# The last stage starts with a quarter of w1, each matmul waits for its own operand, and half of the inverse sums is made in attention's end

## The chip, the cores and the metric

One core of a Trainium2 chip runs the whole kernel. The metric is device microseconds from launch to end, as a median of runs.

## The reference, cut to what matters

```python
xn = layernorm(x)                                  # x: 4 x 2048 x 256
out = x + attention(xn) + moe(xn)
# attention: 16 heads of 16; out = softmax(q k) v; then @ Wo.T + bo
# moe(xn), 16 experts of 64 hidden units, top 2 of 16, then the 1024 best of 2048 tokens per expert and batch
h = gelu(xg @ w1 + b1)                             # xg: the tokens an expert keeps
outs = scatter_add(h @ w2 + b2)
z = xn + outs
moe = (z - mean(z)) / sqrt(var(z) + 1e-5) * gamma + beta
```

The kernel computes all experts on all tokens and multiplies by a mask, so gathering and scattering fall away.

## The kernel before, in words

Four stages, each a block of five instruction streams (PE, DVE, ACT, POOL, SP) that ends with a barrier: `norm` (line 155), `project` (346), `attend` (487) and `finish` (883).

`attend` goes through 64 heads (4 batches of 16). For a head it computes scores, their exponentials and the weighted values; row HD of each group of 32 rows is the softmax's sum. ACT copies the result to the tile `att`, and SP stores it to `att_dram` (`put_att`, line 655). DVE, after its last maxima, makes the 0/1 mask of tokens and experts in the unused part of `v_all` (lines 864 to 875); SP stores it to `mask_b` (707), issues the last head's store (709) and waits for it to land (710). That ends the block (its barrier is at line 563).

`finish` works in 16 blocks of 512 tokens. PE's order for a block, with expert pairs e = 0 to 7 (two experts fill 128 hidden units):
- `hide` (1045): six matmuls of 512 columns (two halves of the features, three products of rounded and remainder parts) into `h_ps`. It runs AHEAD = 2 pairs ahead of `unhide`.
- `unhide` (1059): twelve matmuls on w2 into `o_ps`.
- after pair 5 `hand_out` (1070) spreads the inverse sums over the head's features, and after pair 7 four matmuls add b2 (1103). `project` (1077) multiplies the previous block's attention by Wo.

Between hide and unhide a pair goes through ACT (Gelu, line 1131), DVE (`gate`, 1172, times the mask), ACT again (`g_hi`, 1134, rounded) and POOL (`g_lo`, 1297, the remainder). All buffers of this chain are double.

Ahead of block 0 the weights are prepared. SP loads w1 in four quarters of 256 KB (996), the first block's tokens as `xn_hi` and `xn_lo` (`halves`, 975; 512 KB each), w2 in two halves of 512 KB (999), masks, the sums of all heads (1002), the second block's halves, then waits for b2's split and loads the three parts of b2 (1008). ACT rounds each piece (1148), DVE takes the remainder (1245), POOL splits b2 and Wo (1286 to 1292). DVE then inverts all sums (1250) and splits the inverse into three bf16 parts, half by half, which SP stores to `inverse_dram` (1011). PE waits once, ahead of everything, for b2's rows, the spread matrix and Wo's parts (1106 to 1108).

SP's order for a block is `step` (1015): the halves of the next block, `quotients` (980, this block's attention numerators and inverses), then masks of this block and the next, with the tokens (968) between them. `masks(blk, q)` loads pairs 2q and 2q+1 in two DMAs into one of two buffers, each after the gates that last used it. SP issues in program order, so one wait holds all that stands behind it.

## Time and profile before

| | us |
|---|---|
| median of 3 runs | 3444.11 (3443.16 to 3446.69) |
| the profiled execution | 3444.21 |
| its span, first to last instruction | 3442.4 |
| busy: PE, DVE, ACT, POOL | 3296.2, 2894.2, 2526.4, 929.1 |
| mean granted clock of PE | 0.978 |

The span is what the profile shows of one execution. Of the timeline, stage `finish` runs from 2966.86 us to the end. Times of rows are from the span's start; "idle before <-" names what ended an engine's wait. A queue (SPq) row is the issue of a DMA, not its transfer.

### The profile page before, as it was taken

How to read it: one execution, taken by the hardware profiler on the slowest of the kernel's cores; microseconds unless marked ns; L12 is line 12 of the kernel's file. 1: busy time of each engine (PE TensorE's matmuls, PEld its weight loads, DVE VectorE, ACT ScalarE, POOL GpSimd, SP SyncE). 2: the span in 40 equal slices, each digit the busy share in tenths (PEclk: the TensorE clock that was granted, in tenths of full speed). 3: DMA queues.
4: the chain of work that ended last, by engine and by line, in shares of the span. 5: the costliest groups of instructions: out<-in, count | busy, mean ns of one | idle time of the engine just before them, and what ended most of it. 6: DMA issues, size and time to landing. Idle time of an engine off the chain costs nothing. (4 is left out here: it accounts for less than half of the span.)

```text
span 3442.4 us, 74610 instructions
## 1 busy us (share of the span) xinstructions
PE 3296.2 (96%) x20848; PEld 1706.4 (50%) x20848; DVE 2894.2 (84%) x2987; ACT 2526.4 (73%) x5726; POOL 929.1 (27%) x1339
## 2 busy tenths in 40 slices
PE   7868999999999999999999999999999999599998
PEld 6424444444444444444444444444444444288887
DVE  7508999999999999999999999999999998267777
ACT  3452888888888888888888888888888888443433
POOL 2550222222222222222222222222222222144443
PEclk9986999999999999999999999999999999799999
DMA  6581111122111211111121111211111121355553
GB/s 198 173 241 33 50 54 54 54 60 59 58 56 55 56 56 55 54 54 54 54 60 56 56 55 54 63 56 56 55 54 54 54 59 47 112 136 169 160 164 117
DMA packets 133063, 272.29 MB, mean 79 GB/s; under 512 B 22512, under 2 KB 68656, under 8 KB 120432
## 3 DMA queue, kind: packets, MB, share of 16 engines
q1 hardware_dynamic: 130464, 266.68, 26.7%
q8 instruction: 176, 2.88, 0.4%
q10 hardware_dynamic: 2256, 1.36, 0.2%
q14 instruction: 167, 1.37, 0.1%
HBM read 173.59 MB, written 84.93 MB: 75 GB/s over the span
## 5 line engine op out<-in xcount | busy, mean ns | idle before, releaser
L852 DVE TENSOR_REDUCE half_max<-m_ps 128x1 f32<-128x1024 f32 x2048 | 2413.4, 1220 | 324.5 <-PE m_ps L771 308.8
L724 ACT ACTIVATE prob<-s_ps 128x512 f32<-128x512 f32 (+1 forms) x5120 | 2188.3, 520 | 425.8 <-PE s_ps L781 423.2
L781 PE MATMUL s_ps<-q_feat,k_feat 50*128 50x512 f32 (+1 forms) x5120 | 1538.0, 396 | 7.5 <-issue 4.7
L771 PE MATMUL m_ps<-k_feat,q_feat 48*128 48x512 f32 x4096 | 1405.1, 448 | 55.9 <-DMA k_feat<-k_parts 28.4
L781 PEld LDWEIGHTS s_ps<-q_feat,k_feat 50*128 50x128 f32 x5120 | 796.2, 184 | 983.3 <-ACT prob L724 870.6
L790 PE MATMUL a_ps<-prob,v_head 128*32 128x512 f32 x8192 | 1091.6, 605 | 0.0
L771 PEld LDWEIGHTS m_ps<-k_feat,q_feat 48*128 48x128 f32 x4096 | 616.3, 187 | 287.5 <-DVE half_max L852 248.6
L579 POOL TENSOR_TENSOR shift<-row_max,shift 128x16 fp32r<-128x16 f32 x64 | 14.2, 222 | 1213.0 <-ACT shift L731 1213.0
L790 PEld LDWEIGHTS a_ps<-prob,v_head 128*32 128x32 f32 x8192 | 161.2, 108 | 253.7 <-issue 211.7
L1134 ACT ACTIVATE g_hi<-g 128x512 fp32r<-128x512 f32 x128 | 81.0, 632 | 243.8 <-DVE g L1172 199.8
L1297 POOL TENSOR_TENSOR g_lo<-g,g_hi 128x512 fp32r<-128x512 f32 x128 | 173.0, 1352 | 229.2 <-ACT g_hi L1134 229.2
L606 POOL TENSOR_SCALAR step_of<-route,cand 64x256 f32<-64x256 f32 x217 | 198.6, 915 | 44.5 <-POOL held L607 38.3
L573 POOL COPY v_head<-v_all 128x256 f32 (+1 forms) x64 | 25.3, 397 | 660.2 <-PE a_ps L790 660.1
L607 POOL TENSOR_TENSOR held<-held,step_of 64x256 f32<-64x256 f32 x217 | 157.6, 726 | 39.8 <-POOL step_of L606 39.8
L1172 DVE TENSOR_TENSOR g<-g,mask_bc 128x512 f32<-128x512 f32 x128 | 133.5, 1043 | 36.0 <-ACT g L1131 30.7
L1067 PE MATMUL o_ps<-w_hi,g_hi 128*128 128x256 f32 x512 | 144.6, 282 | 6.1 <-issue 3.7
L1067 PE MATMUL o_ps<-w_lo,g_hi 128*128 128x256 f32 x512 | 144.3, 282 | 0.0
L1067 PE MATMUL o_ps<-w_hi,g_lo 128*128 128x256 f32 x512 | 143.1, 280 | 0.0
L1056 PE MATMUL h_ps<-xn_hi,w_hi 128*128 128x512 f32 x256 | 105.7, 413 | 32.0 <-DMA b_rows<-b_parts 32.0
L1131 ACT ACTIVATE g<-h_ps,b_col 128x512 f32<-128x512 f32 x128 | 86.2, 674 | 25.7 <-PE h_ps L1056 25.7
L1067 PEld LDWEIGHTS o_ps<-w_hi,g_hi 128*128 128x128 f32 x512 | 96.5, 189 | 12.0 <-issue 7.1
L1056 PE MATMUL h_ps<-xn_lo,w_hi 128*128 128x512 f32 x256 | 102.1, 399 | 0.0
(132 smaller groups left out, 1904.1 us busy)
## 6 DMA issues: line engine op xcount, KB each, us to landing
q_feat<-q_parts SPq DMA_DIRECT2D x128, 256.0 KB
k_feat<-k_parts SPq DMA_DIRECT2D x128, 256.0 KB
q_parts<-parts SPq DMA_DIRECT2D x32, 512.0 KB, 4.8
k_parts<-parts SPq DMA_DIRECT2D x32, 512.0 KB, 4.8
q_feat<-q_parts SPq DMA_DIRECT2D x128, 128.0 KB
k_feat<-k_parts SPq DMA_DIRECT2D x128, 128.0 KB
att_dram<-att SPq DMA_DIRECT2D x64, 256.0 KB, 14.0
mask_bc<-mask_b SPq DMA_DIRECT2D x128, 128.0 KB, 4.4
```

The costliest lines, as they stand in the source:

```text
L606: do(pool.tensor_scalar(step_of[:, :], t["route"][:, c * PART:(c + 1) * PART], bound, None, ALU.is_ge))
L607: do(pool.tensor_tensor(held[:, :], held[:, :], step_of[:, :], ALU.add))
L724: act.activation(prob[tile(r, kt) % R][:, cols(j)], s_ps[slot(r, kt, j) % R][:, wide(j)], ACT.Exp).then_inc(exped, 1)
L771: ins = pe.matmul(m_ps[p % 2][:, k * BLK:(k + 1) * BLK], q_feat[r % 2][LOW, qt * P:(qt + 1) * P], k_feat[r % 2][LOW, key:key + BLK], start ...
L781: pe.matmul(s_ps[slot(r, kt, j) % R][:, wide(j)], k_feat[r % 2][UP, kt * P:(kt + 1) * P], q_feat[r % 2][UP, cols(j)], start=True, stop=Tru ...
L790: ins = pe.matmul(a_ps[qb * VW:(qb + 1) * VW, :], v_head[r % R][:, kt, :], prob[tile(r, kt) % R][:, qb * BLK:(qb + 1) * BLK], start=(kt == ...
L852: dve.tensor_reduce(half_max[r][:, p // 2, p % 2:p % 2 + 1], m_ps[p % 2][:, :], AX.X, ALU.max).then_inc(maxed, 1)
L1056: ins = pe.matmul(h_ps[e % 2][:, :], w, v, start=(c == 0 and k == 0), stop=(c == KC - 1 and k == 2))
L1067: ins = pe.matmul(o_ps[k], v, w[:, e, :], start=(e == 0 and m == 0), stop=False)
L1131: act.activation(g[e % 2][:, :], h_ps[e % 2][:, :], ACT.Gelu, bias=b1_col[:, e:e + 1]).then_inc(gelu, 1)
L1172: dve.tensor_tensor(g[e % 2][:, :], g[e % 2][:, :], mask_bc[q % 2][:, e % QTR, :], ALU.mult).then_inc(gated, 1)
L1297: pool.tensor_tensor(g_lo[e % 2][:, :], g[e % 2][:, :], g_hi[e % 2][:, :].bitcast(F32), ALU.subtract).then_inc(split, 1)
```

## The change

- `attend`: once 48 heads' values are copied and 32 heads are stored, SP loads the sums of the first 32 heads. DVE inverts and splits them after the mask, in `v_all` again, and SP stores the parts. The wait for the last head's store to land leaves `attend`; `att` and its semaphore are made outside the stage, and `finish` waits for it just before it loads the second half of the sums.
- `finish`: the pieces come in the order w1[0], w2[0], w1[1], w1[2], w2[1], w1[3]. SP loads w1[0], the first halves, w2[0], masks(0, 0), the other pieces, masks(0, 1), quotients(0), tokens(0); then it waits for b2's split and loads b2, the sums' second half and halves(1, 1).
- ACT and DVE take three pieces ahead of block 0 and one more after each of its pairs 0 to 2. ACT's warming Gelu stands after the three; it rounds Wo after pair 4. DVE inverts the second half after pair 4 and splits it after pair 5; SP stores it after block 0's step and waits for the store.
- POOL splits b2 after pair 1 and Wo after pair 5 of block 0.
- PE waits for the spread matrix in `hand_out`, for Wo in `project`, for b2 ahead of the b2 matmuls, and in hide and unhide for the pieces by their new places.

```diff
@@ -122,6 +122,8 @@
         minus_half = sb("minus_half", [P, TPB])
+        att = sb("att", [P, BLK])
+        att_out = sem("a_att_out")
@@ -530,7 +532,8 @@
     att_read = sem("a_att_read")
-    att_out = sem("a_att_out")
+    att_out = t["att_out"]
+    sums_in, inv_chain, inverted, inverse_stored = sem("a_sums_in"), sem("a_inv_chain"), sem("a_inverted"), sem("a_inverse_stored")
     staged = sb("staged", [P, BLK], F32R)
@@ -544,6 +547,8 @@
     mask16 = spare[0:B * E, 3 * S:3 * S + S // 2].bitcast(BF16)
+    sums = spare[:, 4 * S:4 * S + BLK]
+    inv_parts = spare[:, 4 * S + BLK:4 * S + BLK + PARTS * BLK // 2].bitcast(BF16).rearrange("p (k s) -> p k s", k=PARTS)
     TREE = 8
@@ -698,6 +703,9 @@
                     step(i * U + r, r, half=i * (U // 2) + (r - 1) // 2)
+            sp.wait_ge(v_ready, (B - 1) * H)
+            sp.wait_ge(att_out, 16 * (P // BPS + 1))
+            sp.dma_start(sums, sum_rows(t, 0)).then_inc(sums_in, 16)
             for g in range(1 + ROUNDS * U, HEADS):
@@ -705,9 +713,12 @@
             sp.dma_start(t["mask_b"], mask16).then_inc(mask_stored, 16)
+            sp.wait_ge(inverted, 1)
+            sp.dma_start(t["inverse_dram"][0:P], inv_parts).then_inc(inverse_stored, 16)
             sp.wait_ge(mask_stored, 16)
+            sp.wait_ge(inverse_stored, 16)
+            sp.wait_ge(att_out, 16 * HEADS)
             put_att(HEADS - 1)
-            sp.wait_ge(att_out, 16 * (HEADS + 1))
@@ -873,6 +884,14 @@
             dve.tensor_copy(mask16, gt).then_inc(masked, 1)
+
+            dve.wait_ge(sums_in, 16)
+            do = Chain(dve, inv_chain)
+            do(dve.reciprocal(sums, sums))
+            for k in range(PARTS - 1):
+                do(dve.tensor_copy(inv_parts[:, k, :], sums))
+                do(dve.tensor_tensor(sums, sums, inv_parts[:, k, :], ALU.subtract))
+            dve.tensor_copy(inv_parts[:, PARTS - 1, :], sums).then_inc(inverted, 1)
@@ -925,8 +944,11 @@
     w2_raw = [sb(f"w2_raw{k}", [P, EP // 2, D]) for k in range(2)]
-    pieces = [*([(w1_raw[q], w1_hi[:, :, w1_cols[q]], w1_lo[:, :, w1_cols[q]])] for q in range(4)),
-              *([(flat(w2_raw[k]), *(flat(w)[:, k * 2 * BLK:(k + 1) * 2 * BLK] for w in (w2_hi, w2_lo)))] for k in range(2))]
+    w1_pieces = [(w1_raw[q], w1_hi[:, :, w1_cols[q]], w1_lo[:, :, w1_cols[q]]) for q in range(4)]
+    w2_pieces = [(flat(w2_raw[k]), *(flat(w)[:, k * 2 * BLK:(k + 1) * 2 * BLK] for w in (w2_hi, w2_lo))) for k in range(2)]
+    pieces = [w1_pieces[0], w2_pieces[0], w1_pieces[1], w1_pieces[2], w2_pieces[1], w1_pieces[3]]
+    W1_AT, W2_AT = (0, 2, 3, 5), (1, 4)
+    AHEAD_PIECES = 3
     piece_in = [sem(f"e_piece_in{k}") for k in range(len(pieces))]
@@ -992,25 +1014,30 @@
             w2_rows = t["w2"].rearrange("(c p) n -> p c n", p=P)
-            for q in range(4):
-                sp.dma_start(w1_raw[q], w1_rows[:, :, w1_cols[q]]).then_inc(piece_in[q], 16)
+
+            def load_w1(q):
+                sp.dma_start(w1_raw[q], w1_rows[:, :, w1_cols[q]]).then_inc(piece_in[W1_AT[q]], 16)
+
+            def load_w2(k):
+                sp.dma_start(w2_raw[k][:, :, :], w2_rows[:, 4 * k:4 * k + 4, :]).then_inc(piece_in[W2_AT[k]], 16)
+
+            load_w1(0)
             halves(0, 0)
-            for k in range(2):
-                sp.dma_start(w2_raw[k][:, :, :], w2_rows[:, 4 * k:4 * k + 4, :]).then_inc(piece_in[4 + k], 16)
+            load_w2(0)
             masks(0, 0)
-            for half in range(2):
-                sp.dma_start(sums[:, half, :], sum_rows(t, half)).then_inc(sums_in, 16)
+            load_w1(1)
+            load_w1(2)
+            load_w2(1)
+            load_w1(3)
             masks(0, 1)
+            quotients(0)
             tokens(0)
-            halves(1, 1)
             sp.wait_ge(b2_split, 1)
...
                 sp.dma_start(b2_rows[k * E:(k + 1) * E, :], b2_parts[:, k, :]).then_inc(b2_placed, 16)
-            for half in range(2):
-                sp.wait_ge(sums_inverted, half + 1)
-                sp.dma_start(t["inverse_dram"][half * P:(half + 1) * P], inv_parts[:, :, :]).then_inc(inverses_stored, 16)
-                sp.wait_ge(inverses_stored, 16 * (half + 1))
-            quotients(0)
+            sp.wait_ge(t["att_out"], 16 * (HEADS + 1))
+            sp.dma_start(sums[:, :], sum_rows(t, 1)).then_inc(sums_in, 16)
+            halves(1, 1)
@@ -1030,6 +1057,9 @@
             step(0, 0, first=True)
+            sp.wait_ge(sums_inverted, 1)
+            sp.dma_start(t["inverse_dram"][P:2 * P], inv_parts[:, :, :]).then_inc(inverses_stored, 16)
+            sp.wait_ge(inverses_stored, 16)
             with sp.Fori(0, NBLK // 2 - 1) as i:
@@ -1046,7 +1076,7 @@
                     pe.wait_ge(xn_in[u], (blk // 2 + 1) * 32)
-                pe.wait_ge(piece_split, 1 + e // 2)
+                pe.wait_ge(piece_split, 1 + W1_AT[e // 2])
                 pe.wait_ge(gelu, n + 1)
@@ -1057,7 +1087,7 @@
             def unhide(blk, u, e):
-                pe.wait_ge(piece_split, 5 + e // 4)
+                pe.wait_ge(piece_split, 1 + W2_AT[e // 4])
                 pe.wait_ge(split, blk * EP + e + 3)
@@ -1068,6 +1098,7 @@
             def hand_out(blk):
+                pe.wait_ge(spread_chain, 4)
                 pe.wait_ge(num_in, (blk + 1) * 16 * NUM_LOADS)
@@ -1075,6 +1106,7 @@
             def project(blk):
+                pe.wait_ge(wo_split, 1)
                 pe.wait_ge(num_split, blk + 1)
@@ -1098,14 +1130,12 @@
                         hand_out(blk)
+                pe.wait_ge(b2_placed, 16 * PARTS)
                 pe.wait_ge(loaded, (blk + 1) * 48)
...
-            pe.wait_ge(b2_placed, 16 * PARTS)
-            pe.wait_ge(spread_chain, 4)
-            pe.wait_ge(wo_split, 1)
             for e in range(AHEAD):
@@ -1120,7 +1150,6 @@
             act.dma_start(woT_sb[:, :, :], t["woT"].rearrange("(c p) n -> p c n", p=P)).then_inc(wo_in, 16)
-            act.activation(t["warm"][:, :], t["ident"][:, 0:1], ACT.Gelu)
             act.sem_inc(gelu, 2)
@@ -1133,30 +1162,34 @@
-            def block_step(blk, u, following=True):
+            def round_piece(k):
+                src, hi, lo = pieces[k]
+                act.wait_ge(piece_in[k], 16)
+                act.activation(hi, src, ACT.Copy).then_inc(piece_rounded, 1)
+
+            def block_step(blk, u, first=False):
                 for e in range(EP):
                     hidden_units(blk, e)
+                    if first and AHEAD_PIECES + e < len(pieces):
+                        round_piece(AHEAD_PIECES + e)
+                    if first and e == 4:
+                        act.wait_ge(wo_in, 16)
+                        act.activation(wo_hi[:, :, :], woT_sb[:, :, :], ACT.Copy).then_inc(wo_rounded, 1)
                     if e == EP - 1:
...
             act.sem_inc(projected, 2)
-            for k, piece in enumerate(pieces):
-                act.wait_ge(piece_in[k], 16 * len(piece))
-                for src, hi, lo in piece:
-                    ins = act.activation(hi, src, ACT.Copy)
-                ins.then_inc(piece_rounded, 1)
-                if k == 1:
-                    act.wait_ge(wo_in, 16)
-                    act.activation(wo_hi[:, :, :], woT_sb[:, :, :], ACT.Copy).then_inc(wo_rounded, 1)
+            for k in range(AHEAD_PIECES):
+                round_piece(k)
+            act.activation(t["warm"][:, :], t["ident"][:, 0:1], ACT.Gelu)
             act.wait_ge(small_in, 16 * 3)
-            act.wait_ge(piece_split, 5)
-            block_step(0, 0)
+            block_step(0, 0, first=True)
             with act.Fori(0, NBLK // 2 - 1) as i:
...
                     block_step(i * 2 + 1 + u, 1 - u)
-            block_step(NBLK - 1, 1, following=False)
+            block_step(NBLK - 1, 1)
@@ -1220,9 +1253,32 @@
+            def split_piece(k):
+                src, hi, lo = pieces[k]
+                dve.wait_ge(piece_rounded, k + 1)
+                dve.tensor_tensor(lo, src, hi.bitcast(F32), ALU.subtract).then_inc(piece_split, 1)
+
+            do = Chain(dve, inv_chain)
+
+            def invert_sums():
+                dve.wait_ge(sums_in, 16)
+                do(dve.reciprocal(sums[:, :], sums[:, :]))
+
+            def split_inverses():
+                for k in range(PARTS - 1):
+                    do(dve.tensor_copy(inv_parts[:, k, :], sums[:, :]))
+                    do(dve.tensor_tensor(sums[:, :], sums[:, :], inv_parts[:, k, :], ALU.subtract))
+                dve.tensor_copy(inv_parts[:, PARTS - 1, :], sums[:, :]).then_inc(sums_inverted, 1)
+
             def gates(blk, u, last=True, following=True):
...
                     gate(blk, e)
+                    if not last and AHEAD_PIECES + e < len(pieces):
+                        split_piece(AHEAD_PIECES + e)
+                    if not last and e == 4:
+                        invert_sums()
+                    if not last and e == 5:
+                        split_inverses()
                     if last and e == AHEAD - 1:
@@ -1239,24 +1295,8 @@
-            for k, piece in enumerate(pieces):
-                dve.wait_ge(piece_rounded, k + 1)
-                for src, hi, lo in piece:
-                    ins = dve.tensor_tensor(lo, src, hi.bitcast(F32), ALU.subtract)
-                ins.then_inc(piece_split, 1)
-            dve.wait_ge(small_in, 16 * 3)
-            dve.wait_ge(sums_in, 32)
-            do = Chain(dve, inv_chain)
-            do(dve.reciprocal(sums[:, :, :], sums[:, :, :]))
-            for half in range(2):
-                if half:
-                    dve.wait_ge(inverses_stored, 16)
-                left = sums[:, half, :]
-                for k in range(PARTS - 1):
-                    do(dve.tensor_copy(inv_parts[:, k, :], left))
-                    do(dve.tensor_tensor(left, left, inv_parts[:, k, :], ALU.subtract))
-                dve.tensor_copy(inv_parts[:, PARTS - 1, :], left).then_inc(sums_inverted, 1)
-            dve.wait_ge(piece_split, 6)
+            for k in range(AHEAD_PIECES):
+                split_piece(k)
             gates(0, 0, last=False)
@@ -1281,16 +1321,6 @@
             pool.wait_ge(spread_chain, 4)
-            pool.wait_ge(small_in, 16 * 3)
-            chain = Chain(pool, b2_chain)
-            chain(pool.tensor_copy(b2_parts[:, 0, :], b2_sb[:, :]))
-            chain(pool.tensor_tensor(b2_left[:, :], b2_sb[:, :], b2_parts[:, 0, :], ALU.subtract))
-            chain(pool.tensor_copy(b2_parts[:, 1, :], b2_left[:, :]))
-            pool.tensor_tensor(b2_parts[:, 2, :], b2_left[:, :], b2_parts[:, 1, :], ALU.subtract).then_inc(b2_split, 1)
-            pool.wait_ge(b2_split, 1)
-            pool.wait_ge(wo_rounded, 1)
-            pool.tensor_tensor(wo_lo[:, :, :], woT_sb[:, :, :], wo_hi[:, :, :].bitcast(F32), ALU.subtract).then_inc(wo_split, 1)
-
             def split_units(blk, e):
@@ -1302,11 +1332,29 @@
+            def split_b2():
+                pool.wait_ge(small_in, 16 * 3)
+                chain = Chain(pool, b2_chain)
+                chain(pool.tensor_copy(b2_parts[:, 0, :], b2_sb[:, :]))
+                chain(pool.tensor_tensor(b2_left[:, :], b2_sb[:, :], b2_parts[:, 0, :], ALU.subtract))
+                chain(pool.tensor_copy(b2_parts[:, 1, :], b2_left[:, :]))
+                pool.tensor_tensor(b2_parts[:, 2, :], b2_left[:, :], b2_parts[:, 1, :], ALU.subtract).then_inc(b2_split, 1)
+                pool.wait_ge(b2_split, 1)
+
+            def split_wo():
+                pool.wait_ge(wo_rounded, 1)
+                pool.tensor_tensor(wo_lo[:, :, :], woT_sb[:, :, :], wo_hi[:, :, :].bitcast(F32), ALU.subtract).then_inc(wo_split, 1)
+                pool.wait_ge(wo_split, 1)
+
             def block_step(blk, last=True):
...
                         invert(blk - 1)
+                    if not last and e == 1:
+                        split_b2()
+                    if not last and e == 5:
+                        split_wo()
```

## Rows read from the trace of the kernel before

**Rows 1.** The page's first part: engine, busy time, share of the span, instructions.

```profile
PE 3296.2 (96%) x20848; PEld 1706.4 (50%) x20848; DVE 2894.2 (84%) x2987; ACT 2526.4 (73%) x5726; POOL 929.1 (27%) x1339
```

**Rows 2.** Timeline of PE: its first matmuls of the last stage, and the second block's start.

```profile
2993.30 0.80 PE L1056 MATMUL h_ps<-xn_hi,w_hi 128*128 128x512 f32 x1 [32.03 <-DMA b_rows<-b_parts]
...
3003.72 0.36 PE L1067 MATMUL o_ps<-w_hi,g_hi 128*128 128x256 f32 x1 [3.66 <-issue]
...
3027.24 0.61 PE L1103 MATMUL o_ps<-b_rows,mask_rows 48*128 48x256 bf16 x4
```

**Rows 3.** Windows: us, busy PE, PEld, DVE, ACT, POOL, granted clock, DMA share, GB/s.

```profile
2966.80:2973.30 6.50, 0.00 (x0) 0.00 (x0) 1.01 (x2) 2.74 (x4) 1.70 (x4) 0.50 0.56 161
2973.30:2983.20 9.90, 0.00 (x0) 0.00 (x0) 2.95 (x4) 2.72 (x4) 3.35 (x5) 0.50 1.05 328
2993.30:2996.50 3.20, 3.20 (x8) 2.52 (x9) 2.38 (x5) 0.10 (x1) 0.00 (x0) 0.50 0.00 0
3054.60:3081.35 26.75, 26.75 (x176) 23.71 (x175) 19.77 (x30) 10.73 (x18) 12.35 (x11) 1.00 0.61 163
```

**Rows 4.** Instructions of line 563 (attention's end) and line 193 (first stage's end).

```profile
L563 SPq COMPARE_BRANCH  x1: 49/49/49, 2964.0 to 2964.0; - x1
L563 SPq DRAIN  x1: 68/68/68, 2966.6 to 2966.6; - x1
...
L193 ACTq DRAIN  x1: 1496/1496/1496, 92.8 to 92.8; - x1
```

**Rows 5.** Timeline of SP's queue: attention's last store, then the last stage.

```profile
2962.02 0.34 SPq L657 DMA_DIRECT2D att_dram<-att  x1
2966.86 1.95 SPq L996 DMA_DIRECT2D w_raw<-in_w  x4
...
2969.36 1.94 SPq L978 DMA_DIRECT2D xn_lo<-tok_all  x1
...
2981.65 1.86 SPq L1008 DMA_DIRECT2D b_rows<-b_parts  x3
...
3005.58 19.06 SPq L965 DMA_DIRECT2D mask_bc<-mask_b  x8
```

**Rows 6.** DMA issues of three narrow windows: KB each, us from issue to landing.

```profile
xn_lo<-tok_all SPq DMA_DIRECT2D x1, 512.0 KB, 10.1
...
xn_lo<-tok_all SPq DMA_DIRECT2D x1, 512.0 KB, 6.7
...
mask_bc<-mask_b SPq DMA_DIRECT2D x1, 128.0 KB, 5.3
```

**Rows 7.** Timeline of ACT in the last stage's beginning.

```profile
2968.87 1.28 ACT L1123 ACT_TABLE_LOAD   x1 [6.94 <-issue]
2970.16 0.20 ACT L1123 ACTIVATE warm<-ident 128x1 f32<-128x1 f32 x1
2970.89 0.63 ACT L1148 ACTIVATE w_hi<-w_raw 128x512 fp32r<-128x512 f32 x1 [0.53 <-DMA w_raw<-in_w]
```

**Rows 8.** Timeline of DVE: mask chain's end, first split, the inverses, first gate.

```profile
2925.06 1.22 DVE L875 CAST v_all<-v_all 64x2048 bf16<-64x2048 f32 x1
2971.55 0.69 DVE L1245 TENSOR_TENSOR w_lo<-w_raw,w_hi 128x512 fp32r<-128x512 f32 x1 [45.27 <-ACT w_hi L1148]
...
2986.43 6.55 DVE L1250 RECIPROCAL sums<-sums 128x1024 f32<-128x1024 f32 x1 [0.65 <-DMA sums<-att_dram]
...
2995.39 0.43 DVE L1258 CAST inv_parts<-sums 128x512 bf16<-128x512 f32 x1
...
3000.94 0.68 DVE L1172 TENSOR_TENSOR g<-g,mask_bc 128x512 f32<-128x512 f32 x1
```

**Rows 9.** Timeline of POOL: the first and the fourth instruction that split b2.

```profile
2975.57 0.39 POOL L1286 CAST b_parts<-b_sb 16x256 bf16<-16x256 f32 x1 [6.79 <-DMA gamma_bc<-in_gamma]
...
2977.23 0.66 POOL L1289 TENSOR_TENSOR b_parts<-b_left,b_parts 16x256 bf16<-16x256 f32 x1
```

**Rows 10.** Waits of SP's queue, 2955 to 3030 us: total, times, longest.

```profile
SPq L656 <- ACT att L736: 28.0, 1, 28.0
```

4 lines of the change are left out of this document (2 added, 2 removed).

## The prediction

> **What bounds the kernel now.** I read the page's first part first: PE is busy 96% of the span, all other engines less [rows 1]. So time comes off only where PE stands still, or where it waits in the chain. PE's own timeline shows one large hole: its first matmul of the last stage starts at 2993.30 after 32.03 us of idleness [rows 2]. Behind it the last stage is a stream: between 3054.60 and 3081.35 PE is busy 26.75 of 26.75 us, and that is one block [rows 3]. All of the change lies in the hole and in the first block behind it; the other 15 blocks end as much earlier as the first one does.
>
> What ends the hole: PE waits for all three b2 rows. Their DMAs are issued from 2981.65 [rows 5] and stand behind everything issued before. What would end it next, if each matmul waited only for its own operand, is the question. Two marks serve for the sum: PE's first matmul on w2 at 3003.72, and the b2 matmul that ends block 0's sums at 3027.24 [rows 2]. Between them lie 23.5 us. The last stage starts at 2966.86 with SP's first load [rows 5]. I call the new start T and count from there.
>
> **The barrier.** SP issues attention's last store at 2962.02 for 0.34 us, waits for its landing, branches at 2964.0 and only reaches its drain at 2966.6 [rows 4, 5]. The change drops the wait for the landing. The 2.8 us from the branch to the first load stay. T = 2962.36 + 2.8 = 2965.2, a gain of 1.7. Bounds: 0 (something else holds the barrier) and 4.3 (the 2.6 us before the drain go too). I take 1.7, since the landing is what the trace has in front of the branch.
>
> **First operands.** Before, xn_lo was issued sixth, behind 1.05 MB of w1 and the 0.5 MB of xn_hi, and landed 10.1 us after its issue, 12.6 after the start [rows 5, 6]. Now it is third, issued near T+1. Lower bound: in the running stage the same load lands after 6.7 us [rows 6], so T+7.7. Upper: T+12.6. I take T+9.2: 1.7 MB (first w1 quarter, both halves of xn, ACT's 0.4 MB) at a rate between the 161 and 328 GB/s of the two windows [rows 3], and the 2 us that attention's last store needed to land. The first w1 quarter was rounded at 2970.89, T+4.0, and split by T+5.4 [rows 7, 8], earlier. PE's clock is granted at 0.50 there, 1.2 GHz, with 8 matmuls in 3.2 us [rows 3]; it will be after 13 us of idleness as well. Two hides of six matmuls take 2.6 us each: the first ends at T+11.8.
>
> **ACT's order is the next bound.** ACT now rounds three pieces (w1's first quarter, w2's first half, w1's second) before the Gelu table is loaded. Behind xn_lo come w2's half, two masks and that quarter, 1.05 MB: at 328 GB/s [rows 3] 3.2 us, so T+12.4. Rounding takes 0.63; the table load and the warming instruction span 2968.87 to 2970.36, 1.5 us [rows 7]. Before, these hid behind the first landing; now they lie on the path. First Gelu at T+14.5, its end and the first gate at T+15.2. From the first gate to the first w2 matmul took 3000.94 to 3003.72, 2.8 us [rows 2, 8]. So the first w2 matmul comes at T+18.0 = 2983.2, which is 20.5 us earlier than before.
>
> The load's row shows 1.28 us and the next instruction 0.01 us behind it [rows 7], but it came after ACT had issued DMAs, not behind running work. The Trainium skill (ScalarE: Activation LUTs, What ACT_TABLE_LOAD costs) counts a drain of some 1.4 us beside it, 2.66 us for each switch of set. By it, this load behind three roundings would cost that much more than the row, and the whole time would be 1.4 us longer. No row here has a drain beside a load, so the sum goes by the row.
>
> **Block 0, new waits.** ACT and DVE each take one more piece after the first three experts. A step is gate 0.7, g_hi 0.63, rounding 0.63, Gelu 0.7 and some 0.3 of hand-overs: 3.0 us. The w2 half is twice as wide, rounding and split some 1.1 and 1.2 (doubled from 0.63 and 0.69 less a fixed part [rows 7, 8]): 3.9. Gates stand at T+15.2, 18.2, 22.1, 25.1; the fifth would follow at T+27.5.
>
> It won't, because SP is held. SP waits for b2's split before it loads b2's rows, the sums, the second block's halves and then the masks of experts 4 and 5. POOL splits b2 only after its second g_lo, which ends near T+21.1. The four instructions take 2975.57 to 2977.89, 2.3 us [rows 9]: T+23.4. SP then needs 1.9 for b2 [rows 5], 0.5 for the sums, 1.1 for the halves: the two masks are issued from T+27.0. With 1 MB just ahead of them they land late: the row for a mask behind halves says 5.3 us after issue [rows 6], xn_lo's 10.1 behind a full backlog is the other end. I take 6.0 after the second issue: T+33.6. Everything SP issued before (some 5.3 MB) needs about 20 us at these rates and is through by then. So **the fifth gate waits some 6 us for its masks**, a wait that kernel before does not have (its SP was free at 3005.58 [rows 5]).
>
> After it, DVE inverts the second half of the sums: half of 6.55, 3.3 us, then, after the next gate, the split of 2992.98 to 2995.82, 2.8 us [rows 8]. Gates: T+33.7, 38.0, 41.8, and 44.6 behind the division. The eighth w2 group starts at T+47.4, takes 1.4 and the b2 matmul comes at T+48.9 = 3014.1 (before: 3027.24). The gain is **13.1 us**; of the 20.5, 7.4 are given back in block 0 (6 by the masks, the rest by the inversion and the pieces). POOL's split of wo (1.3 us, after the sixth g_lo) fits into the slack of a 2.8 us step.
>
> **At nothing.** In attention's end one DMA more reads the sums and one stores the inverses; SP waits 28.0 us there for ACT's last copy [rows 10], and DVE is idle 45.27 us behind its mask chain [rows 8] for 3.3 + 2.8 of new work. Were that cover gone, 6 us would be due. PE's three waits per block that stood once ahead of the blocks: its sequencer runs ahead of matmuls in a stream that is busy 26.75 of 26.75 us with waits in every group [rows 3], so 0. If they cost, 48 waits at 0.05 us are 2.4. The start-up issues (18 against 19 ahead of the b2 wait) end by T+14 and hide before T+23.4. Behind block 0 SP stores the inverses and waits some 3 us: last masks out at T+46, landed inverses T+49, halves and quotients T+52.6, the next masks issued by T+53.9 and landed 5.3 later at T+59.2. They are wanted 4/8 of 26.75 = 13.4 us after the block's start, T+62.3. Hidden, by 3 us; if that fails it is a rival below.
>
> **Sum.** The profiled execution took 3444.21 us, span 3442.4 and 1.8 around it, 0.1 above the median 3444.11. 3444.2 less 13.1 is 3431.1; I forecast 3431.
>
> **Rivals.**
> (a) No mask wait: the masks land before T+28, as POOL comes to b2 sooner or the queues are empty. For it: 5.3 us is a loaded landing. Against: SP's own issues put them at T+27 already. The inversion of the sums stays. Gain 5 more: 3426.
> (b) ACT drains before it switches tables. Where ACT ended a stage behind running work, its drain took 1.50 us [rows 4]; one of these on the path gives 3432.6. For it stands that the load now follows ACTIVATEs; against, that the load's row shows nothing around it. The Trainium skill's rule above is this rival, at nearly the same price.
> (c) Late operands: xn_lo at its upper bound T+12.6 and all behind it 3.4 later; or PE, busy in short bursts, stays at 1.2 GHz [rows 3] through block 0. Gain 8 to 10: 3435.
> (d) Both (c) and a mask landing like the 10.1 of a full backlog: 3444.2 - 13.1 + 3.4 + 4.1 = 3438.6, no change.
> (e) Slower: SP stays late. It runs through one fixed order per block, masks behind halves and quotients; if its 3 us of lateness isn't caught up, the fifth gate of every block waits. Break-even is 13.1 / 15 = 0.9 us per block; at 1.5 it gives 3453.6. Against it: the eight mask loads of block 0 span 19.06 us of SP's time [rows 5], of which issuing is 8 x 0.6; the rest is waiting for gates and absorbs 3 us.
> That the change doesn't do what it says would be PE's first matmul still waiting for b2; the moved waits exclude it.
>
> **How the numbers follow.** Forecast 0.50, (a) 0.15, (b) 0.10, (c) 0.12, (d) 0.08, (e) 0.05. A measurement can tell 0.2%, 6.9 us. (a), (b), (c) and the forecast are faster by more: 0.87. Same 0.08, slower 0.05. The range goes from 3424 (a, with the earlier barrier) to 3437 (c at its worst), leaving out (d), (e) and the tails.
>
> **What would show it.** Right: the last stage starts near 2965.2; PE's first matmul there 9 us later, no longer released by the b2 rows; first w2 matmul near 2983; a table load between third rounding and first Gelu; the fifth gate of block 0 idle some 6 us, ended by a mask DMA; a reciprocal of 128x512 with 3.3 us behind it; the b2 matmul near 3014; then 26.75 us per block. Wrong: no idle time before the fifth gate (a); blocks above 26.75 us (e); PE still at 0.50 after T+20 (c).

## The result, and the profile after

| | before | after |
|---|---|---|
| median, one comparison | 3445.11 (3443.16 to 3447.10, 12 runs) | 3437.53 (3433.69 to 3440.66, 12 runs) |
| profiled execution | 3444.21 | 3436.23 |
| its span | 3442.4 | 3434.5 |

The ratio is 0.9977, interval 0.9969 to 0.9986: 7.6 us faster (interval 4.8 to 10.7), by more than the 0.2% that can be told, where I had 13.1. The time lies 0.5 us above the end of my range.

The same marks as in the prediction: T is SP's first load of the last stage, gates and the b2 matmul of block 0 are counted from T, "stage" is the span less T, and "block 1" goes from block 0's b2 matmul to the next one.

| | forecast | after | before |
|---|---|---|---|
| T | 2965.2 | 2963.72 | 2966.86 |
| PE's first matmul | +9.2 | +8.4 | +26.4 |
| first gate | +15.2 | +15.6 | +34.1 |
| first w2 matmul | +18.0 | +18.5 | +36.9 |
| fifth gate | +33.7 | +35.6 | +45.1 |
| b2 matmul of block 0 | +48.9 | +52.2 | +60.4 |
| block 1 | 26.75 | 29.81 | 26.75 |
| stage | 464.1 | 470.8 | 475.5 |

The start went as forecast. The stage is 6.7 us longer than forecast: 3.3 us of it arose in block 0, behind the fourth gate, 3.1 in block 1, where I had put nothing, and the rest behind it.

**The start.** PE's timeline, changed kernel; to be held against [rows 2]:

```profile
2972.08 0.79 PE L1086 MATMUL h_ps<-xn_hi,w_hi 128*128 128x512 f32 x1 [12.79 <-DMA xn_lo<-tok_all]
...
2982.21 0.55 PE L1097 MATMUL o_ps<-w_hi,g_hi 128*128 128x256 f32 x1
...
3015.87 0.61 PE L1136 MATMUL o_ps<-b_rows,mask_rows 48*128 48x256 bf16 x4
```

xn_lo now ends the hole, and the hole is 12.79 instead of 32.03 us. ACT's timeline there, against [rows 7]:

```profile
2976.49 0.63 ACT L1168 ACTIVATE w_hi<-w_raw 128x512 fp32r<-128x512 f32 x1 [0.68 <-DMA w_raw<-in_w]
2977.14 1.28 ACT L1186 ACT_TABLE_LOAD   x1
2978.44 0.20 ACT L1186 ACTIVATE warm<-ident 128x1 f32<-128x1 f32 x1
2978.55 0.67 ACT L1160 ACTIVATE g<-h_ps,b_col 128x512 f32<-128x512 f32 x1
```

The rounding ends at 2977.12 and the table load starts at 2977.14; nothing stands between them. The Trainium skill (ScalarE: Activation LUTs, What ACT_TABLE_LOAD costs) counts a drain of some 1.4 us beside a load of 1.28; the trace agrees on the load and shows no drain.

**The fifth gate.** SP's queue, against [rows 5]:

```profile
2960.05 0.33 SPq L662 DMA_DIRECT2D att_dram<-att  x1
2963.72 0.40 SPq L1019 DMA_DIRECT2D w_raw<-in_w  x1
...
2988.93 1.86 SPq L1037 DMA_DIRECT2D b_rows<-b_parts  x3
...
2992.55 20.59 SPq L987 DMA_DIRECT2D mask_bc<-mask_b  x8
3013.18 0.59 SPq L1061 DMA_DIRECT2D inverse_dram<-inv_parts  x1
3017.44 0.41 SPq L998 DMA_DIRECT2D xn_hi<-tok_hi_dram  x1
```

POOL's timeline of the same moments, against [rows 9]:

```profile
2985.25 1.38 POOL L1338 CAST b_parts<-b_sb 16x256 bf16<-16x256 f32 x1
2986.71 1.00 POOL L1339 TENSOR_TENSOR b_left<-b_sb,b_parts 16x256 f32<-16x256 f32 x1
```

And DVE's, against [rows 8]:

```profile
2979.32 0.69 DVE L1205 TENSOR_TENSOR g<-g,mask_bc 128x512 f32<-128x512 f32 x1 [1.48 <-ACT g L1160]
...
2984.91 1.47 DVE L1259 TENSOR_TENSOR w_lo<-w_raw,w_hi 128x1024 fp32r<-128x1024 f32 x1 [1.65 <-ACT w_hi L1168]
...
2999.32 0.69 DVE L1205 TENSOR_TENSOR g<-g,mask_bc 128x512 f32<-128x512 f32 x1 [8.19 <-DMA mask_bc<-mask_b]
2999.93 3.34 DVE L1265 RECIPROCAL sums<-sums 128x512 f32<-128x512 f32 x1
...
3005.09 1.38 DVE L1269 CAST inv_parts<-sums 128x512 bf16<-128x512 f32 x1
3006.51 1.66 DVE L1270 TENSOR_TENSOR sums<-sums,inv_parts 128x512 f32<-128x512 f32 x1
...
3028.99 0.69 DVE L1205 TENSOR_TENSOR g<-g,mask_bc 128x512 f32<-128x512 f32 x1 [3.33 <-issue]
```

The predicted wait for masks is there, 8.2 us. SP asks for the fifth gate's masks at T+28.8 (forecast T+27.0), since POOL's split of b2 took 3.65 us, from 2985.25 to 2988.90, instead of 2.3: its first cast took 1.38 instead of 0.39 and ended within 0.3 us of DVE's w_lo subtraction. The landings are right to a tenth: 5.3 and 6.0 us after their issues from 2992.55 on (the DMA view of that moment gives the median of the two), and the gate runs as the second lands:

```profile
mask_bc<-mask_b SPq DMA_DIRECT2D x2, 128.0 KB, 5.7
```

**Block 1.** The last DVE row is the one that I had not foreseen. It is block 1's fourth gate. It waits 3.33 us for nothing that a semaphore shows, and PE runs dry behind it. Windows of block 1 and block 2 of the changed kernel (us, busy PE, PEld, DVE, ACT, POOL, clock, DMA share, GB/s):

```profile
3015.90:3045.70 29.80, 27.02 (x176) 23.55 (x176) 19.81 (x30) 10.60 (x18) 12.30 (x10) 1.00 0.54 149
3045.70:3072.40 26.70, 26.70 (x175) 23.69 (x174) 19.77 (x30) 10.68 (x18) 12.36 (x10) 1.00 0.57 163
```

It happens once: in block 2 PE is busy throughout again. Block 1 is the first block that the engines run from their loops (`Fori`); block 0's code stands ahead of them. The DMA view lists a queue "q14 instruction" that carries code. Its first packet of block 1, in the kernel before (3035.7 to 3036.0, 8.6 us behind the b2 matmul):

```profile
DMA packets 1, 0.01 MB, mean 27 GB/s; under 512 B 0, under 2 KB 0, under 8 KB 0
q14 instruction: 1, 0.01, 7.5%
```

and in the changed kernel (3026.8 to 3027.1, 11.1 us behind it):

```profile
DMA packets 36, 0.04 MB, mean 137 GB/s; under 512 B 3, under 2 KB 35, under 8 KB 35
q1 hardware_dynamic: 35, 0.03, 50.8%
q14 instruction: 1, 0.01, 9.8%
```

Before, it moves alone, over queues already empty. After, it comes 2.5 us later and among 35 data packets: those of block 2's halves and block 1's quotients and masks, which SP issues from 3017.44 on, 1.6 us behind the b2 matmul, where it was 2.2 us ahead of it before. From the b2 matmul to the stall, DVE's own instructions stand at the same distance from that matmul in both kernels, within 0.2 us. SP is that late because it stores the inverses at 3013.18 and waits for the landing. The gate starts 2.0 us after the packet. That the gate waits for this packet is read from their times; no row names it as the releaser. The Trainium skill (Runtime: NRT & Kernel Launch, Instruction fetch mechanics) says that each engine fetches its code in blocks of 16 KiB over a DMA queue of its own, and that crossing from one block to the next is mostly hidden. Block 1 has two packets of 0.01 MB on that queue, in line with the size; hidden it was in the kernel before, and not here, where DVE stood still for 3.33 us.

### The profile page after: what moved, and what is told of

It is laid out like the page before. It is cut to its first block and busy times, and to the rows that moved or that the text cites. A ratio compares the mean times of both kernels' runs of the same rounds, so it can differ in the third digit from the quotient of the medians.

```text
span 3434.5 us, 74611 instructions
## 1 busy us (share of the span) xinstructions
PE 3299.8 (96%) x20848; PEld 1708.6 (50%) x20848; DVE 2898.2 (84%) x2988; ACT 2525.7 (74%) x5726; POOL 932.6 (27%) x1339
## 5 line engine op out<-in xcount | busy, mean ns | idle before, releaser
L584 POOL TENSOR_TENSOR shift<-row_max,shift 128x16 fp32r<-128x16 f32 x64 | 14.3, 223 | 1211.2 <-ACT shift L742 1211.2
L1097 PE MATMUL o_ps<-w_hi,g_hi 128*128 128x256 f32 x512 | 145.6, 284 | 13.7 <-POOL g_lo L1327 13.7
L1086 PE MATMUL h_ps<-xn_hi,w_hi 128*128 128x512 f32 x256 | 106.1, 414 | 15.3 <-DMA xn_lo<-tok_all 12.8
L1086 PE MATMUL h_ps<-xn_hi,w_lo 128*128 128x512 f32 x256 | 102.0, 398 | 0.0
```

What stands on the lines that cost most here:

```text
L1086: ins = pe.matmul(h_ps[e % 2][:, :], w, v, start=(c == 0 and k == 0), stop=(c == KC - 1 and k == 2))
L1097: ins = pe.matmul(o_ps[k], v, w[:, e, :], start=(e == 0 and m == 0), stop=False)
```

## The experiments

Theory A: the forecast's mechanism holds; 2 to 3 us were lost in block 0 to POOL's late b2 split and DVE's slowed inversion split, and 3 in block 1 to late code behind late data. Rival B: block 1's hole is a fixed cost of the new code's length or place. Rival C: the barrier or PE's added waits cost what is missing.

All results; rows in one group ran beside the same runs of the kernel before. The stage is that of each profiled execution.

| run | median | ratio (interval) | first gate | fifth gate | b2 matmul | block 1 | stage |
|---|---|---|---|---|---|---|---|
| before: 3446.47 | | | | | | | |
| changed, again | 3440.02 | 0.9979 (0.9970, 0.9988) | 15.7 | 34.9 | 51.4 | 30.46 | 470.3 |
| store early | 3437.10 | 0.9971 (0.9960, 0.9982) | 15.3 | 35.8 | 52.4 | 27.14 | 469.3 |
| b2 early | 3433.26 | 0.9963 (0.9949, 0.9976) | 15.4 | 30.7 | 47.3 | 29.04 | 464.9 |
| warm first | 3437.81 | 0.9972 (0.9961, 0.9982) | 14.0 | 33.1 | 49.6 | 31.33 | 469.4 |
| before: 3446.76 | | | | | | | |
| before, again | 3446.33 | 0.9999 (0.9989, 1.0009) | 34.1 | 44.0 | 58.9 | 26.75 | 474.9 |
| waits only | 3446.47 | 1.0001 (0.9992, 1.0011) | 34.5 | 46.5 | 61.8 | 26.75 | 477.2 |
| masks first | 3432.49 | 0.9955 (0.9941, 0.9969) | 16.3 | 28.4 | 45.5 | 31.06 | 465.5 |
| landing kept | 3440.62 | 0.9979 (0.9970, 0.9988) | 17.0 | 37.3 | 53.8 | 28.79 | 471.1 |
| before: 3446.64 | | | | | | | |
| reordered | 3427.89 | 0.9946 (0.9933, 0.9960) | 14.4 | 26.6 | 43.7 | 26.93 | 459.0 |
| sums inverted first | 3429.48 | 0.9950 (0.9937, 0.9964) | 17.1 | 29.3 | 43.7 | 26.79 | 460.2 |
| stored twice | 3442.07 | 0.9984 (0.9975, 0.9993) | 15.9 | 35.7 | 52.3 | 30.44 | 471.7 |
| before: 3445.70 | | | | | | | |
| sums second | 3426.18 | 0.9942 (0.9929, 0.9956) | 16.4 | 28.5 | 42.9 | 26.76 | 458.7 |

Attention's end moves by up to 5.5 us from one execution to the next (PE's last matmul there ends between 2959.29 and 2964.78), whatever the kernel. So a theory is judged by the stage, and by medians only with their intervals.

The stage moves too, by PE's granted clock. In the last block PE stands still for 2.40 us in all fourteen profiles. Behind that hole it is granted 2.4 GHz throughout in some and 1.2 for a while in others, and the same block takes 26.61 or up to 27.85 us. Windows of the last block of the version with all reorderings and of the one with the store early, and of block 1 of the changed kernel's repeat:

```profile
3385.38:3411.99 26.61, 24.21 (x163) 21.52 (x162) 18.99 (x29) 10.05 (x16) 12.31 (x10) 1.00 0.33 104
```

```profile
3391.74:3419.59 27.85, 25.45 (x164) 22.67 (x163) 18.99 (x29) 10.03 (x16) 12.30 (x10) 0.95 0.30 99
```

```profile
3019.21:3049.67 30.46, 28.54 (x175) 24.99 (x175) 19.19 (x30) 10.82 (x18) 12.29 (x10) 0.94 0.52 145
```

Block 1 was granted 0.94 or 0.95 in three profiles (changed again, warm first, masks first), behind PE holes of 1.9 to 2.8 us, and 1.00 in all others, one with a hole of 3.4 us among them. In the repeat's block 1 PE was busy for 28.54 us, in the first profile's for 27.02, with as many matmuls within one. So 1.2 to 1.5 us of a block in a single profile can be the clock and not the edit.

**Both kernels again.** No edit.

> The changed kernel once more, for a second profile. Theory A (code of DVE comes late because the data transfers of block 1 come late, a thing of the program's order): the idle 3.3 us with no releaser ahead of DVE's gate of pair 3 in block 1 is there again, within 1 us, and PE loses some 2.8 us to it. Theory B (chance of one execution): it is not there, or at another place. Both expect the fifth gate of block 0 to wait 8 us for its masks, and a time near 3437.5.

> The kernel before once more, for a second profile. If attention itself varies from one execution to the next, its last matmul ends up to 2 us away from 2961.3, as it did in the five profiles of the changed kernels (2959.3 to 2963.8), while the stage behind it takes 475.5 within 0.5. If the kernel before has DVE's idle time without a releaser in block 1 too, it shows here; I expect none, and blocks of 26.75 from the second on.

Stages repeat: 470.8 and 470.3, 475.5 and 474.9, in part by luck: in the kernel before, block 0 took 1.5 us less the second time and the last block 0.9 more. Block 1 is longer both times in the changed kernel, by 3.06 and 3.71 us. DVE's stall was 3.33 us and then 2.48; the second time 1.5 us of the 3.71 are the clock's. The stage gives 4.8 us of the gain; the barrier gives 1.2. In the changed kernel's first profile PE left attention 2.0 us earlier than in the first of before, which no edit explains; the two repeats are 0.3 us apart.

**PE's waits alone.** On the kernel before:

```diff
             def hand_out(blk):
+                pe.wait_ge(spread_chain, 4)
...
             def project(blk):
+                pe.wait_ge(wo_split, 1)
...
                         hand_out(blk)
+                pe.wait_ge(b2_placed, 16 * PARTS)
...
-            pe.wait_ge(b2_placed, 16 * PARTS)
-            pe.wait_ge(spread_chain, 4)
-            pe.wait_ge(wo_split, 1)
```

> The kernel before with one part of the change alone: PE waits for b2, the spread matrix and Wo where it uses them, and no longer ahead of everything. Theory 1 (the three waits are what holds PE 32 us): PE's first matmul comes with xn_lo, near T+12.7 instead of T+26.4, and the stage is up to 13 us shorter. Theory 2 (DVE holds the first gate: it ran at 3000.94, right behind the last cast of the inverses at 2995.82 and 3001.0, and no PE wait changes that): the first matmul is as early as in theory 1, but the first gate stays at T+34.1, the first w2 matmul at T+36.9, and the whole time within 1 us of before (3446).

Nothing is gained: 1.0001. PE's and DVE's timelines of that kernel:

```profile
2981.51 0.80 PE L1056 MATMUL h_ps<-xn_hi,w_hi 128*128 128x512 f32 x1 [18.38 <-DMA xn_lo<-tok_all]
...
3006.05 0.55 PE L1067 MATMUL o_ps<-w_hi,g_hi 128*128 128x256 f32 x1 [16.87 <-issue]
```

```profile
3002.91 0.43 DVE L1258 CAST inv_parts<-sums 128x512 bf16<-128x512 f32 x1
3003.26 0.68 DVE L1172 TENSOR_TENSOR g<-g,mask_bc 128x512 f32<-128x512 f32 x1
```

PE's first matmul comes 13.7 us earlier, and the first gate at T+34.5 as ever, directly behind the last cast of the inverses. So "PE waits for all three b2 rows" names what ended PE's hole and not what bounded the stage: that was DVE's program order, inverses ahead of gates. The change gains by moving the inversion; that the waits had to move with it is argued, since no run moves the inversion alone. The 48 added waits leave the blocks from block 1 on at 26.75 (the last at 26.71).

The stage is even 1.7 to 2.2 us longer. PE starts early, then stands still for 16.87 us, and is granted 1.2 GHz behind it, where the kernel before had 0.80 and 1.00 in the same stretch of its two profiles:

```profile
3003.30:3011.70 8.40, 5.65 (x20) 5.10 (x21) 3.14 (x4) 3.20 (x6) 3.81 (x3) 0.50 0.44 141
```

**The landing kept.** On the changed kernel, at attention's end:

```diff
             put_att(HEADS - 1)
+            sp.wait_ge(att_out, 16 * (HEADS + 1))
```

> The changed kernel, with the wait for the last store's landing back in attention's end. From that store's issue to the last stage's first load it was 4.84 us before and 3.67 and 3.69 in the two profiles after. If the removed wait is what made the difference, it is 4.8 again and the time is 1.2 us longer than the changed kernel (3441); if the 2.5 us of SP ahead of its drain overlap with the landing in another way, it stays at 3.7.

SP's queue, with the wait:

```profile
2964.52 0.33 SPq L662 DMA_DIRECT2D att_dram<-att  x1
2969.33 0.40 SPq L1020 DMA_DIRECT2D w_raw<-in_w  x1
```

From the last store to the first load: 4.81 us with the wait (4.84, 4.90 and 4.92 in the three profiles of before and of the waits alone), 3.67 and 3.69 in the changed kernel. The barrier's part is 1.2 us. In the medians it does not stand out (ratios 0.9979 and 0.9979).

**The store of the inverses ahead of the last masks:**

```diff
                 for q in range(4):
+                    if q == 3 and first:
+                        sp.wait_ge(sums_inverted, 1)
+                        sp.dma_start(t["inverse_dram"][P:2 * P], inv_parts[:, :, :]).then_inc(inverses_stored, 16)
...
-            sp.wait_ge(sums_inverted, 1)
-            sp.dma_start(t["inverse_dram"][P:2 * P], inv_parts[:, :, :]).then_inc(inverses_stored, 16)
             sp.wait_ge(inverses_stored, 16)
```

> SP stores the second half's inverses ahead of the last two mask loads of block 0, so that the landing is over when they are issued, and block 1's halves, quotients and masks go out some 3 us earlier. Theory A: DVE's idle time of 3.3 us with no releaser in block 1 goes, PE streams through block 1 without its 2.8 us hole, and the time falls by 2.8 us (3434.7). Theory B (the hole does not depend on SP's order): hole and time stay within 1 us (3437.5). A third: the last masks of block 0 are now late, block 1 waits for them, and the time rises.

Its gate in block 1, and the code packet (3025.2 to 3025.5, 8.7 us behind the b2 matmul, near the 8.6 of the kernel before):

```profile
3027.22 0.70 DVE L1206 TENSOR_TENSOR g<-g,mask_bc 128x512 f32<-128x512 f32 x1 [0.63 <-issue]
```

```profile
q14 instruction: 1, 0.01, 6.4%
```

SP is 2.3 us ahead of the b2 matmul again, the packet moves alone, the stall falls from 3.33 to 0.63, block 1 from 29.81 and 30.46 to 27.14. Rival B falls: the code is as long and, but for these lines, in the same place. Of these 3 us the stage of this profile keeps 1.3, as its last block took 27.85 us at a granted clock of 0.95; the median lies 2.9 us below the changed kernel's beside it.

The fourteen profiles fall into two groups. In seven (the kernel before twice, waits only, store early, reordered, and both with the sums inverted ahead) SP issues block 2's halves 2.2 to 2.3 us ahead of the b2 matmul, the packet comes 8.5 to 8.7 us behind it, and block 1 takes 26.75 to 27.14. In the other seven SP issues them 1.4 to 4.3 us behind it, the packet comes 10.1 to 11.7 us behind it, DVE stalls for 2.3 to 4.0 us, and block 1 takes 28.79 to 31.33.

**The inverses stored twice** (SP made later on purpose):

```diff
             sp.wait_ge(inverses_stored, 16)
+            sp.dma_start(t["inverse_dram"][P:2 * P], inv_parts[:, :, :]).then_inc(inverses_stored, 16)
+            sp.wait_ge(inverses_stored, 32)
```

> The changed kernel, with the store of the inverses and the wait for its landing done twice behind block 0: 3 us more of lateness of SP. Theory A: block 1's halves, quotients and masks go out 3 us later, DVE's idle time without a releaser grows from 2.5 to 3.3 us to some 6, block 1 from 29.8 to 30.5 to some 33, and the time by 2 to 3 us (3441). Theory B (not SP's order): block 1 as in the changed kernel, time the same. If instead the gates of block 1 wait for a mask DMA by name, the lateness acts through the masks and not through code.

Waits of DVE in block 1 (total, times, longest):

```profile
DVE g L1207 <- issue: 4.0, 1, 4.0
```

SP's loads come 4.3 us behind the b2 matmul instead of 1.6, the packet 11.7 us behind it instead of 11.1, the stall is 4.0, the longest of all, and block 1 takes 30.44. That is no longer than in the changed kernel's repeat, but there 1.5 us were the clock's; of the late profiles with a granted clock of 1.00 (28.79, 29.04, 29.81) it is longer by 0.6 us or more. The gate again starts 2.1 us after the packet. Direction right, size well short: the packet is not held until SP's data are through, since those now end 1 to 2 us after it. In all nine profiles with a stall the gate starts 1.7 to 2.1 us after the packet. That SP's order makes the stall is shown by the edits; that it does so through the code is inferred from these times, and by what rule data delay the packet stays open.

**b2 split ahead of POOL's first g_lo:**

```diff
-                    if not last and e == 1:
-                        split_b2()
...
+            split_b2()
             block_step(0, last=False)
```

> POOL splits b2 ahead of block 0, as before the change; all else is the changed kernel. Theory of the prediction (SP is held by the wait for b2's split, and the masks of pairs 4 and 5 go out late): SP passes the wait by T+14, those masks are issued right after the second gate, near T+20, the fifth gate's wait of 8.2 us falls under 1 us, and the whole time by 5 to 7 us (3431). Rival (the transfers themselves are the bound, SP's wait only hides it): the masks land no earlier than T+32, the wait moves by 2 us at most, the time by under 2 us.

```profile
2997.32 0.69 DVE L1205 TENSOR_TENSOR g<-g,mask_bc 128x512 f32<-128x512 f32 x1 [4.49 <-DMA mask_bc<-mask_b]
```

The fifth gate and the b2 matmul come 4.1 to 4.9 us earlier, and the stage is 5.6 us shorter. The rest of the wait, 4.5 us, is not POOL's: the masks are asked for from 19.3 us after T on, and land 7.5 and 10.6 us after their issues, behind 1 MB of the second block's halves and what was queued before it. (The 9.1 that the next expectation names is the median of the two.)

**b2 early, and those halves and tokens behind the fifth gate's masks:**

```diff
             quotients(0)
-            tokens(0)
...
-            halves(1, 1)
...
                         masks(blk + q // 2, (q + 2) % 4)
+                    if q == 0 and first:
+                        halves(1, 1)
+                        tokens(0)
```

> The kernel with b2 split early, and beside it SP loads the masks of pairs 4 and 5 ahead of the first block's tokens and the second block's halves (2.1 MB). With b2 alone split early these masks went out 9.5 us sooner, yet their landing took 7.5 to 9.1 us and the fifth gate still waited 4.5 us, at T+30.7. Theory (queue: what SP issued ahead of them holds them): they land some 4 us after issue, near T+24, the fifth gate is at T+28 without a wait, and the stage is 2.7 us shorter than with b2 alone (462.2 against 464.9 from T to the end); the whole time near 3431. Rival (DVE is late in any case): the fifth gate stays within 0.5 us of T+30.7, and nothing is gained.

No wait for masks is left; the fifth gate follows the fourth after 2.0 us. The b2 matmul comes at T+45.5, 1.7 us earlier than with b2 alone, yet the stage is no shorter: block 1 took 31.06 instead of 29.04. The stall accounts for 0.6 of these 2.0 us (3.17 after 2.57); PE's clock, granted at 0.95 in this block and at 1.00 in the other, for 1.5. The expected 2.7 us are neither shown nor excluded: against their own runs of before the medians gained 14.3 and 13.2.

**The warming Gelu ahead of the pieces:**

```diff
             act.sem_inc(projected, 2)
+            act.activation(t["warm"][:, :], t["ident"][:, 0:1], ACT.Gelu)
             for k in range(AHEAD_PIECES):
                 round_piece(k)
-            act.activation(t["warm"][:, :], t["ident"][:, 0:1], ACT.Gelu)
```

> The warming Gelu stands ahead of the three pieces, as before the change. If ACT's order was the bound of the first gate, as predicted, table load and warming (1.5 us) hide behind the first landing, the first gate comes at T+14.1 instead of T+15.6, and by the forecast the whole time falls by up to 1.5 us. Rival: the fifth gate waits for its masks in any case, SP's issue of them hangs on POOL's second g_lo and moves with it by 1.5, so block 0 ends 1.5 earlier; if instead the masks' landing is bound by transfers, block 0 ends where it did and the time stays within 0.5 us.

```profile
2970.20 1.28 ACT L1184 ACT_TABLE_LOAD   x1 [5.76 <-issue]
2971.50 0.20 ACT L1184 ACTIVATE warm<-ident 128x1 f32<-128x1 f32 x1
...
2980.69 0.64 ACT L1168 ACTIVATE w_hi<-w_raw 128x512 fp32r<-128x512 f32 x1 [0.78 <-DMA w_raw<-in_w]
2981.24 0.66 ACT L1160 ACTIVATE g<-h_ps,b_col 128x512 f32<-128x512 f32 x1
```

The first Gelu stands directly behind the third rounding and the first gate at T+14.0, 1.6 us earlier: the 1.5 us that the prediction put on the path. With a drain it would have been 3. Block 1 is the longest seen, at 31.33, with the same stall of 3.33 us as in the changed kernel's first profile and a granted clock of 0.95.

**All four reorderings together** (store, b2, masks and Gelu as above, without the doubled store).

> Four reorderings of the changed kernel together, each tried alone or in a pair before: b2 split ahead of block 0, masks of pairs 4 and 5 ahead of tokens and second halves, inverses stored ahead of the last masks, warming Gelu first. Theory A (DVE's code comes late because block 1's data go out late): the idle time without a releaser in block 1 falls under 1 us, block 1 takes under 27.5 us (31.1 with the first two alone), and with the first gate 1.6 us earlier the stage from T to the end is near 461 (465.5 with the first two alone); the time near 3428. Theory B (the hole comes from DVE's place in its code, however early data go): block 1 stays at 29 to 31 us, the stage near 464, the time near 3431.

The two windows are its block 1 and block 2:

```profile
3010.66:3037.60 26.94, 26.94 (x176) 23.57 (x175) 19.84 (x30) 10.64 (x18) 12.32 (x10) 1.00 0.58 158
3037.60:3064.35 26.75, 26.75 (x176) 23.71 (x175) 19.76 (x30) 10.74 (x18) 12.36 (x10) 1.00 0.56 162
```

3427.9 is 18.8 us below the kernel before. The stage is 11.5 us shorter than the changed kernel's (470.5, the mean of two), and the parts one by one gave only 7.5: 1.3 the store, 5.6 b2, 1.2 the Gelu, and the masks on top of b2 a loss of 0.6. That looks as if they helped one another, but a good part is the clock: 1.2 us of the store's last block, and 1.5 of block 1 in the Gelu's and the masks' profiles. By medians the parts add up. Beside the changed kernel's 3440.02 the store gave 2.9, b2 6.8 and the Gelu 2.2, and the masks 1.1 on top of b2, 13.0 in all; together they gave 12.3 beyond the repeat's 6.5. No run shows more than a sum.

**The sums inverted before the first gate.** As all four, but SP loads the sums behind xn and stores their inverses behind b2, and DVE inverts them after its first piece:

```diff
             halves(0, 0)
+            sp.wait_ge(t["att_out"], 16 * (HEADS + 1))
+            sp.dma_start(sums[:, :], sum_rows(t, 1)).then_inc(sums_in, 16)
...
-            for k in range(AHEAD_PIECES):
+            split_piece(0)
+            invert_sums()
+            split_inverses()
+            for k in range(1, AHEAD_PIECES):
                 split_piece(k)
```

> As the four reorderings, but the second half of the sums is loaded behind xn and inverted by DVE ahead of block 0, between its first and second piece, where DVE waits for data. Then the gates of pairs 5 and 6 lose the 1.2 and 2.4 us by which they exceed 2.8, block 0 is 3 us shorter behind its first gate; the 256 KB ahead of w2 and the second w1 quarter make the first gate up to 1.5 later. Net 1 to 3 us faster than the reordered kernel (3425 to 3427). Rival: the split of the inverses ends later than the second piece is rounded, so the first gate is 3 us later and nothing is gained.

A miss. The sums were in DVE's hands only at T+9.2, the inverses done at T+15.4, and the first gate came at T+17.1. From first gate to b2 matmul it is 26.6 us instead of 29.3, as the inversion is out of the stream; the two cancel, and the b2 matmul comes at T+43.7 in both. The stage's other 1.2 us are its last block, 27.85 at a granted clock of 0.94.

**The same, the sums loaded ahead of xn** (the two added lines stand above `halves(0, 0)`).

> T is the issue of SP's first load of the last stage. As the version with the sums inverted first, but the sums (256 KB) go out ahead of xn instead of behind its first two pieces. If what cost that version 2.6 us at the first gate was the late landing of the sums (T+9.2), they now land near T+5.5 and are inverted by about T+12, beside the wait for the second piece: first gate near T+15.4, block 0 behind it 26.6 us as there, its b2 matmul near T+42, the stage 457 to 458 us, the time near 3426. Rival: the sums ahead delay xn, w2 and the second quarter by 1 us or more, or the inversion still ends behind the second piece: first gate at T+16.5 or later, the stage 459 to 460 us, the time 3428 to 3429.5, no better than the four reorderings together.

PE's first matmul, and DVE's last cast of the inverses:

```profile
2977.22 0.80 PE L1087 MATMUL h_ps<-xn_hi,w_hi 128*128 128x512 f32 x1 [15.81 <-DMA xn_lo<-tok_all]
```

```profile
2976.72 0.77 DVE L1272 CAST inv_parts<-sums 128x512 bf16<-128x512 f32 x1
```

The inverses are ready at T+11.8, as expected, but 256 KB ahead of xn cost PE's first matmul 3.3 us (T+11.5) and the first gate 2.0. The rival was right on the delay, the expectation on block 0 (26.6 behind the gate), and the stage of 458.7 lies between the two. The time of 3426.2 came out as expected, but in the profiled execution 1.2 us of it is attention's earlier end; the stage is 0.3 us shorter than with the four reorderings, and the ratios 0.9942 and 0.9946 can't be told apart. Either is the best version.

## Why the prediction was off, step by step

- **What bounds the kernel**: half right. PE's hole was where the time lay, but removing its wait alone gains nothing; DVE's inversions ahead of the gates held the stage at T+34.
- **The barrier**: 1.2 us instead of 1.7; inside its bounds.
- **First operands, ACT's order**: right. T+8.4 for 9.2, first gate T+15.6 for 15.2, w2 T+18.5 for 18.0. The table load cost its 1.3 us with no drain, so rival (b) falls, and with it, for this load, the figure of the Trainium skill. Windows of PE's clock, in the changed kernel:

```profile
2984.00:2999.30 15.30, 10.36 (x62) 8.38 (x60) 4.99 (x4) 4.39 (x7) 7.57 (x7) 1.00 0.61 172
2999.30:3007.50 8.20, 5.34 (x22) 4.90 (x23) 8.05 (x7) 2.93 (x5) 4.03 (x3) 0.58 0.12 31
```

  It was at 2.4 GHz by T+20, so (c) falls. Behind the mask wait, in which PE was idle for 5.6 us, it was granted mostly 1.2 again; but DVE is busy 8.05 of 8.20 us there and sets the pace, and with the masks first, where there is no such wait, the gates from the sixth on are as far apart (5.25 us to the seventh in both). There PE was granted 1.00:

```profile
3000.20:3005.50 5.30, 4.43 (x28) 3.28 (x27) 5.16 (x7) 1.21 (x2) 2.89 (x2) 1.00 0.26 49
```

- **Block 0**: mechanism right, sizes short by 3.3 us (2.5 in the repeat). "The four instructions take 2.3 us": 3.65 beside DVE's work, and the fifth gate 1.9 late. "The split, 2.8 us": 4.7 from 3003.91 to 3008.63, as two instructions took 1.38 and 1.66 instead of 0.43 and 0.69, the first while POOL made a g_lo, the second while it split Wo. All nine profiles with the split in this place repeat it; with the sums inverted ahead of the first gate, and POOL idle, the split took 0.43 and 0.69 an instruction. "Fits into the slack" was true of POOL and false of DVE. I took durations from rows in which the other engine stood idle.
- **The step that failed** is under "At nothing": "Behind block 0 SP stores the inverses and waits some 3 us ... Hidden, by 3 us." The masks were indeed in time, and SP did catch up, so rival (e) did not come. But I had asked only whether a buffer would be late. What came late, by the times of the packets, was the code for DVE's loop. DVE stalled for 3.33 and 2.48 us, and block 1 was 3.1 and 3.7 us longer, 1.5 of the latter by PE's clock behind its hole; with the store earlier it was 0.4 longer.
- **Sum**: 13.1 less 0.5 (barrier), 3.3 or 2.5 (block 0) and 3.1 or 3.7 (block 1) leaves 6.2 to 6.4; measured were 7.6 and 6.5 in medians, whose intervals reach some 3 us to either side.

## What to carry to other kernels

The wait that ends an engine's hole is not its bound: ask what the next engine had in front of its first useful instruction. Price an instruction that moves next to another engine's work from a row where that engine is busy. Where a program enters a loop, late transfers may delay the code; a store that is put off costs there what no buffer shows. And before a fix is priced from one profile, compare the granted clock of each block: here the clock alone made 1.2 us in blocks that no edit had touched.

## What the runs showed that I had not expected

- Code comes through DMA queues of its own, and its first packet of the loop moved 8.5 to 8.7 us behind the b2 matmul over idle queues, 10.1 to 11.7 us behind it among data. DVE stalled for at most 0.6 us in the first case and for 2.3 to 4.0 us in the second, and went on 1.7 to 2.1 us after the packet.
- Small instructions of POOL and DVE stretch beside each other: 0.39 to 1.38 us for a cast of 16x256, 0.69 to 1.66 for a subtraction of 128x512. The Trainium skill (GPSIMD Engine Reference, Key points) names a shared interface and contention with DVE instructions that are in a 2-port mode or have two inputs in SBUF; the first cast here agrees with it, next to such a subtraction. The stretched cast on DVE has a single input, and which condition it met was not tried.
- The same mask loads landed 5.3 and 6.0 us after their issues behind 1 MB, and 7.5 and 10.6 us after it when the backlog of the start-up still stood ahead of them.
- Behind a hole of PE of the same length the granted clock fell in some executions and not in others: the last block, with 2.40 us of hole each time, was granted 0.94 to 1.00 and took 27.85 to 26.61 us.
